# A decoder layer on one core: keys and queries projected for two tiles at a time, in alternate steps

## The reference

```
t  = rms_norm(layer_norm(x)) * rms_w           # self attention, 8 heads of 64
q, k, v = t @ wq, t @ wk, t @ wv
o  = softmax(q k^T / 8, causal) v * sigmoid(t @ w_gates)
x1 = x + o @ wo
x2 = x1 + cross_attention(layer_norm(x1), ctx, mask) @ W_out^T   # 16 heads of 8, tanh-clipped scores
y  = x2 + layer_norm(x2) + experts(...)         # 8 experts, the best 2 of each token
```

## Time and profile before

| what | before |
|---|---|
| median of 3 runs | 259.38 us (257.85 to 260.14) |
| the profiled execution, its own time | 259.18 us |
| its span, first to last instruction | 257.4 us |
| busy PE / PEld / DVE / ACT / POOL | 224.5 / 184.5 / 197.1 / 144.0 / 128.2 us |
| instructions PE / DVE / ACT / POOL | 3360 / 874 / 333 / 184 |
| mean granted TensorE clock | 0.958 |

### The profile page before, as it was taken

The page is one execution under the profiler, slowest core; times in us unless marked ns, Lnnn a source line. Parts: engine busy times, 40 slices in busy tenths (PEclk is TensorE's granted clock), DMA queues, the critical chain, the costliest instruction groups (busy, mean ns, idle before and its releaser), DMA issues. The chain is left out here.

```text
span 257.4 us, 9580 instructions
## 1 busy us (share of the span) xinstructions
PE 224.5 (87%) x3360; PEld 184.5 (72%) x3360; DVE 197.1 (77%) x874; ACT 144.0 (56%) x333; POOL 128.2 (50%) x184
## 2 busy tenths in 40 slices
PE   8888999999999999999999988857987999989800
PEld 2666877886886887877777755436977899989700
DVE  2558687898898889989888897968995777766343
ACT  2455776885776776777667656424332355545400
POOL 1122321413546746646556356636777776656630
PEclk9999999999999999999999999975999999999965
DMA  7995999300000000000000001065774888888376
GB/s 221 254 374 215 401 410 406 135 3 4 3 12 26 14 13 24 14 13 25 13 14 21 16 0 35 24 174 179 218 216 116 268 275 230 268 239 250 94 237 190
DMA packets 24526, 36.31 MB, mean 141 GB/s; under 512 B 3726, under 2 KB 14225, under 8 KB 24224
## 3 DMA queue, kind: packets, MB, share of 16 engines
q1 hardware_dynamic: 20272, 29.98, 36.3%
q0 software_dynamic: 2272, 4.27, 4.7%
q10 hardware_dynamic: 1936, 1.46, 1.9%
HBM read 21.26 MB, written 14.89 MB: 140 GB/s over the span
## 5 line engine op out<-in xcount | busy, mean ns | idle before, releaser
L1959 POOL TENSOR_TENSOR rstd<-var,cst 128x1 f32<-128x1 f32 (+1 forms) x32 | 25.8, 807 | 73.8 <-DVE var L1300 48.7
L2058 POOL DMA_INDIRECT results<-y_sb,meta x39 | 38.3, 981 | 16.9 <-DVE xw_sb L1707 9.1
L505 PE MATMUL six<-gT_sb,gu_sb 128*128 128x128 f32 x312 | 43.3, 288 | 0.6 <-issue 0.6
L505 PEld LDWEIGHTS six<-gT_sb,gu_sb 128*128 128x128 f32 x312 | 39.4, 201 | 1.0 <-issue 0.8
L2016 POOL DMA_INDIRECT slots<-pay,slot_i x32 | 33.2, 1038 | 11.9 <-issue 7.0
L1093 ACT ACTIVATE jsilu<-six 128x256 f32<-128x256 f32 x39 | 14.9, 383 | 21.8 <-PE six L505 21.8
L1690 DVE TENSOR_TENSOR hidT<-jsilu,six 128x256 f32<-128x256 f32 x39 | 16.2, 416 | 10.7 <-PE six L505 10.7
L505 PE MATMUL six<-downT_sb,hidT 128*128 x156 | 23.6, 278 | 0.7 <-DVE hidT L1690 0.7
L1029 ACT ACTIVATE etanh<-six,xscale 128x1024 f32<-128x1024 f32 x16 | 17.8, 1113 | 7.1 <-PE six L505 7.1
L505 PEld LDWEIGHTS six<-downT_sb,hidT 128*128 128x128 f32 x156 | 20.3, 192 | 1.2 <-issue 1.1
L505 PEld LDWEIGHTS six<-wo_sb,oT_sb 128*128 128x128 f32 x128 | 15.5, 191 | 6.4 <-issue 6.4
(11 more groups left out here) (159 smaller groups left out, 537.8 us busy)
## 6 DMA issues: line engine op xcount, KB each, us to landing
gu_sb<-in_guT SPq DMA_DIRECT2D x39, 256.0 KB, 3.7
slots<-empty_sb SPq DMA_DIRECT2D x16, 528.0 KB, 5.9
g_sb<-slots SPq DMA_DIRECT2D x39, 66.0 KB, 3.4
ctxT_all<-in_ctxT SPq DMA_DIRECT2D x1, 1024.0 KB, 8.7
downT_sb<-in_downT SPq DMA_DIRECT2D x1, 1024.0 KB, 9.8
y_all<-results SPq DMA_DIRECT2D x4, 256.0 KB, 3.6
x_all<-in_x SPq DMA_DIRECT2D x2, 320.0 KB, 3.7
results<-y_sb,meta POOLq DMA_INDIRECT x39
```

Source lines behind the costliest of these rows:

```text
L505: return pe.matmul(o, lhsT=l, rhs=r, start=start, stop=stop, **kw)
L1959: nc.gpsimd.tensor_tensor(dst, src, half[:, 0:dst.shape[1]], ALU.pow).then_inc(semaphore, 1)
L2058: nc.gpsimd.indirect_dma_start(results, bass.IndirectOffsetOnAxis(meta[j % (2 * RING)][:, 0:1].bitcast(I32), 0), y_sb[k][:, :], None, boun ...
```

## The change

Two tiles lie side by side in tT_sb ([P, 2, P]), and a product multiplies 128 columns of weights by the 256 columns of both. Fill number n is the keys of tiles n and n+1 where n is even, the queries of tiles n-1 and n where it is odd; step i does fill i+2. So keys and queries alternate from step to step, and each step has four products of 256 columns where it had eight of 128. Half of a fill (two of the four 128-column blocks of weights) goes to ko_bank, half to qp_bank; the two copies of 128 x 512 on ScalarE stay. The loop begins at step -3. `turn_t`, `normalize` and the statistics of x come two steps earlier for the same tile (the statistics now at the ends of odd steps); `turn_t(2)` is put at the end of step -1; the cast of the constants and its wait move from step 0 to -1; the two keep_warm products move to step -2, behind `turn_t(1)`.

TensorE, and the functions that it calls:

```diff
-        tT_sb = several("tT_sb", [P, P])
-        qT_sb = several("qT_sb", [P, NJ, P])
-        k_sb = several("k_sb", [P, NJ, P])
+        tT_sb = several("tT_sb", [P, 2, P])
+        q_sb = several("q_sb", [P, NJ, 2, P], n=2)
+        k_sb = several("k_sb", [P, NJ, 2, P], n=2)
...
-            for i in range(-2, TAIL):
+            for i in range(-3, TAIL):
...
+        def tT(t):
+
+            return tT_sb[t // 2 % BUFS][:, t % 2]
+
+        def query_fill(t):
+
+            return t | 1
...
                 after(pe, t_ready, t)
-                after(pe, egate_ready, t - 1)
+                after(pe, tT_ready, t - 1)
+                after(pe, egate_ready, 0 if t == 2 else t - 3)
                 pe.transpose(tr_ps, t_sb[t % BUFS], ident).then_inc(t_turned, 1)
...
+            def project_pair(n, bank, j0):
+                w = wq_sb if n % 2 else wk_sb
+                both = tT_sb[n // 2 % BUFS].rearrange("p u t -> p (u t)")
+                for m in range(2):
+                    ins = mm(bank[:, m * 2 * P:(m + 1) * 2 * P], w[:, (j0 + m) * P:(j0 + m + 1) * P], both)
+                return ins
+
+            def project_lo(n):
...
+                after(pe, tT_ready, n | 1)
+                after(pe, lo_ready, n - 1)
+                after(pe, oT_ready, n - 3)
+                project_pair(n, ko_bank, 0).then_inc(lo_done, 1)
+
+            def project_hi(n):
+
+                after(pe, hi_ready, n - 1)
+                after(pe, pT_ready, n - 3)
+                after(pe, tanh_ready, n - 4)
+                project_pair(n, qp_bank, NJ // 2).then_inc(hi_done, 1)
...
-                after(pe, qT_ready, t)
-                after(pe, k_ready, t)
+                after(pe, lo_ready, query_fill(t))
+                after(pe, hi_ready, query_fill(t))
...
-                if has(i, -1):
-                    turn_t(i + 1)
+                if has(i, -3) and i != -1:
+                    turn_t(i + 3)
...
-                if i == -1:
+                if i == -2:
                     keep_warm(2, quad[:, 3])
-                if has(i, -1):
-                    project_k(i + 1)
-                    project_q(i + 1)
+                if has(i, -2):
+                    project_lo(i + 2)
+                    project_hi(i + 2)
...
                 if has(i, -1):
                     scores(i + 1)
+                if i == -1:
+                    turn_t(2)
```

ScalarE's step, and its list behind the steps:

```diff
-                if has(i, 0):
-                    evacuate_k(i)
+                if has(i, -1):
+                    evacuate_lo(i + 1)
                 if has(i, 4):
                     turn_xn(i - 4)
-                if has(i, 0):
-                    evacuate_q(i)
+                if has(i, -1):
+                    evacuate_hi(i + 1)
...
-                if has(i, -1):
-                    turn_t(i + 1)
+                if i == 0:
+                    turn_t(2)
+                if has(i, -3) and i != -1:
+                    turn_t(i + 3)
                 if has(i, 0):
                     softmax(i)
...
-            evacuate_q(15)
             turn_xn(11)
-            evacuate_k(15)
```

VectorE's step, and the steps of the statistics:

```diff
-                if i == 0:
+                if i == -1:
                     dve.wait_ge(l_b, 16)
...
-                if has(i, -1):
-                    normalize(i + 1)
+                if has(i, -3):
+                    normalize(i + 3)
...
-XSTEPS = (-1, 0, 2, 4, 6, 8, 10)
+XSTEPS = (-3, -2, 1, 3, 5, 7, 9)
```

More of the change, by code:

```diff
@@ L514, in turn_t @@
                 after(pe, t_ready, t)
-                after(pe, egate_ready, t - 1)
+                after(pe, tT_ready, t - 1)
+                after(pe, egate_ready, 0 if t == 2 else t - 3)
                 pe.transpose(tr_ps, t_sb[t % BUFS], ident).then_inc(t_turned, 1)
-            def project_k(t):
-                if t == 0:
-                    pe.wait_ge(l_wk, 16)
[L522 to L532, removed]
-                    pe.wait_ge(l_wq, 16)
[L534 to L539, removed]
+            def project_pair(n, bank, j0):
[5 more added lines that the diff above has]
+            def project_lo(n):
+                if n == 0:
+                    pe.wait_ge(l_wk, 16)
+                if n == 1:
+                    pe.wait_ge(l_wq, 16)
+                after(pe, tT_ready, n | 1)
[7 more added lines that the diff above has]
+                project_pair(n, qp_bank, NJ // 2).then_inc(hi_done, 1)
             def project_v(t):
@@ L569, in gates @@
                     rows = slice(b * S, (b + 1) * S)
-                    ins = mm(gate_ps[rows], tT_sb[t % BUFS][:, rows], wgate_sb[:, :])
+                    ins = mm(gate_ps[rows], tT(t)[:, rows], wgate_sb[:, :])
                 ins.then_inc(gate_done, 1)
@@ L587, in scores @@
                             rows, cols = slice(a * 64, a * 64 + 64), slice(b * S, (b + 1) * S)
-                            mm(s_ps[cols, a, j], qT_sb[t % BUFS][rows, j, cols],
-                               k_sb[t % BUFS][rows, j, cols], start=(j == 0), stop=False,
+                            mm(s_ps[cols, a, j], q_sb[t // 2 % 2][rows, j, t % 2, cols],
+                               k_sb[t // 2 % 2][rows, j, t % 2, cols], start=(j == 0), stop=False,
                                skip_group_check=True)
@@ L600, in turn_p @@
                 after(pe, weighed, t)
-                if has(t + 1, 0):
-                    after(pe, qT_ready, t + 1)
+                if has(t + 2, 0):
+                    after(pe, hi_ready, t + 2)
                 else:
@@ L615, in attend @@
                 after(pe, v_ready, t)
-                after(pe, k_ready, last(t + 1))
-                if not has(t + 1, 0):
+                after(pe, lo_ready, last(t + 2))
+                if not has(t + 2, 0):
                     after(pe, oT_ready, t - 1)
@@ L686, in turn_a @@
                 after(pe, a_ready, t)
-                after(pe, tT_ready, last(t + 3))
+                after(pe, tT_ready, last(t + 5))
                 after(pe, xnT_ready, t - 1)
@@ L710, in turn_xn @@
                 after(pe, xn_ready, t)
-                after(pe, tT_ready, last(t + 4))
-                if not has(t + 4, 0):
+                after(pe, tT_ready, last(t + 6))
+                if not has(t + 6, 0):
                     after(pe, egate_ready, last(t + 3))
@@ L988, in turn_t, with heads, evacuate_lo, evacuate_hi @@
                 after(act, t_turned, t)
-                nc.scalar.activation(tT_sb[t % BUFS], tr_ps, ACT.Copy,
+                nc.scalar.activation(tT(t), tr_ps, ACT.Copy,
                                      scale=vecs[:, 0:1]).then_inc(tT_ready, 1)
[L993 to L999, removed]
+            def heads(n, j0):
+                pair = (q_sb if n % 2 else k_sb)[n // 2 % 2]
+                return pair[:, j0:j0 + NJ // 2].rearrange("p j u t -> p (j u t)")
+            def evacuate_lo(n):
+                after(act, lo_done, n)
+                copy(heads(n, 0), ko_bank).then_inc(lo_ready, 1)
+            def evacuate_hi(n):
+                after(act, hi_done, n)
+                copy(heads(n, NJ // 2), qp_bank).then_inc(hi_ready, 1)
             def gates(t):
@@ L1017, in turn_p @@
                 after(act, p_turned, t)
-                copy(pT_sb[t % BUFS], qk_ps).then_inc(pT_ready, 1)
+                copy(pT_sb[t % BUFS], pT_ps).then_inc(pT_ready, 1)
             def turn_o(t):
@@ L2021, in x_power @@
             def x_power(i):
-                if i == -1:
+                if i == XSTEPS[0]:
                     pool.wait_ge(l_c, 16)
```

11 lines of the change are left out of this document (5 added, 6 removed).

## The result

The changed kernel takes 267.01 us (median of 4 executions, 263.56 to 269.47), beside 258.91 us for the kernel before on the same chip (257.85 to 260.14). Executions more than 1.5% above the fastest of their kernel, here 268.5 and 269.47 us, do not enter the ratios in this document; the other two, 263.56 and 265.52 us, give a ratio of 1.0216, with a 95% interval of [1.011, 1.0321]. The kernel is slower, as forecast, by more than the 1% that the prediction called its border; whether by 2% the interval leaves open. The forecast time was 262.5 us, the range 259.0 to 265.0: the mean of those two, 264.5 us, lies inside near the top, the median of all four beyond it.

A forecast was written before the change was run, and what follows sets the result against it. TensorE's order was taken to set the pace, VectorE following closely. Lead-in +3.2, steps 1 to 13 -0.9, statistics +1.2 and end -0.2 made +3.3 on 259.18, so 262.5 us, range 259.0 to 265.0 (the forecast's own 261.0 to 264.0).

The forecast's parts named there:

- Lead-in: Before the second scores: two tiles' fills and turns stand ahead on the path, +3.2 us, ends +2.5 and +4.
- Width of a product: TensorE's fills: a record of 256 columns costs what two of 128 cost, 0.215 us, so 1.72 us a step.
- 0.07 a step: Steps 1 to 13: each fill on TensorE 1.72 us instead of 1.79, -0.9 us in all.
- The rival in which the weights set the pace: TensorE's fills: weight loads limit the pace, so wide products make the kernel faster, 256.3 us; chance 7%.
- estimate of 98 ns: TensorE: spacing for 256 columns, between the skill's 81 ns for 128 and 131 for 512; 1.2 times that for 128.
- Statistics of x: Now ahead of even steps on VectorE, delaying turn_xn in steps 6, 8 and 10: +1.2 us, ends 0 and 2.0.
- turn_xn comes 0.40 us late, three times: Steps 6, 8 and 10: 0.81 us of statistics against 0.41 free; cross_attend and values queue behind turn_xn.
- in steps 2 and 4 ... I cost nothing: Steps 2 and 4: no choice of experts stands there, so the moved statistics were costed at nothing.
- The end: Step 14: 1.79 us less TensorE work, but turn_xn waits for VectorE's norm_x, so only -0.2 us.
- The rival in which the delay is given back: Step 14 returns all 1.79 us and the statistics find cover: +0.5, 259.7 us; chance 25%.
- Sum: The whole kernel: +3.2 - 0.9 + 1.2 - 0.2 = +3.3 us, giving 262.5 us.
- The clock rises later: Lead-in: TensorE idle before the clock's rise, first two half fills take twice as long, +1.8, 264.3 us; chance 13%.

The follow-up runs named there:

- lead-in by tile: The changed kernel with its first two fills made for one tile each, by products of 128 columns; 265.56 us, ratio 1.0226.
- combined kernel: The changed kernel with statistics of x at even steps, an unread fill in step 14 and first two fills for one tile each; 262.43 us, ratio 1.0101.
- second profile: The changed kernel run again with nothing changed, profiled at 264.09 us; median 265.1 us, ratio 1.0208.
- place earlier: The changed kernel with VectorE's place written ahead of norm_q instead of behind it; 266.58 us, ratio 1.0206.
- narrow products: The changed kernel with each product of 256 columns done as two of 128 with the same weights; 266.89 us, ratio 1.0309.

## Why the prediction was right in sign and too small

**Lead-in, +3.2 forecast, +3.47 measured: right, step by step.** scores(0) at 12.53 (12.28 forecast), the third fill 2.32 us behind them (2.31), scores(1) at 19.21 (18.93). Most of the 0.25 that is missing lies at the second fill: it begins at 9.78, not 9.60, since the copy that frees its bank starts 0.10 later than reckoned (9.04 against 8.94) and the fill follows the copy's end by 0.14, not 0.05. The lead-in by tile took 1.48 us back where the order was undone, and its profile kept 1.13 of it to the end; in the combined kernel it is not seen at the end.

**Width of a product: right.** A fill takes 69.32 to 71.05 us, from its first product to the next instruction, 1.73 us (1.72 forecast):

```profile
69.32 1.89 PE L512 MATMUL six<-tT_sb,wk_sb 128*128 128x256 f32 x8
71.05 0.27 PE L725 MATMUL turn_bank<-cst,xn_sb 128*128 128x128 f32 x1
```

Eight records in it make 0.216 each, twice the 0.112 of half the width. With the statistics put back the steps up to scores(13) are 0.76 us shorter than before, near the 0.07 a step. The rival in which the weights set the pace is out. The estimate of 98 ns that was worked out from the Trainium skill, "TensorE: Matmul & The Clock Gate", section "Back-to-back issue gap", does not fit either: these float32 records follow each other by 216 ns.

**Statistics of x, +1.2 forecast, 2.4 measured: this term was mis-sized**, above its bound of 2.0 too. What it followed came nearly as written: "turn_xn comes 0.40 us late, three times". Counted from the scores that begin a step, turn_xn starts 0.33, 0.30 and 0.33 us later in steps 5, 7 and 9 than with the statistics at the even steps, and the values queued behind it 0.38, 0.35 and 0.40, together 1.13 of the 1.2. The step that failed is that the prediction stopped there. route, a few products further on, waits for place on the same late VectorE and comes another 0.29, 0.32 and 0.28 us late, 0.89 in all. And "in steps 2 and 4 ... I cost nothing" holds, but step 6, also without a term, is 0.66 us longer, with a wait of 0.56 of the cross attention's scores for VectorE's probs. Less the 0.26 of step 8 this is 1.13 + 0.89 + 0.66 - 0.26 = 2.42. place could have been found in the kernel before, where route once waits 0.2 us for it, in step 13. The size is shown from both sides: by the kernel before with this part alone (2.46 between scores(5) and scores(11)) and by the changed kernel without it (-2.4 in these steps).

**The end, -0.2 forecast, -0.12 at scores(15) and -0.22 at the last instruction from scores(14) on: right.** turn_xn waits 1.46 us for norm_x, and 1.73 us of dead work put there cost 0.70, some 0.4 of them by a wait of the experiment's own. The rival in which the delay is given back is out. In step 13 the changed kernel gains 0.46 that I had not; one part is turn_t, 0.26 us from its start to the next instruction, which no longer stands there as no tile is left to turn.

**Sum.** 3.47 - 0.76 + 2.85 (with the 0.44 in step 4) - 0.46 - 0.22 = 4.88, where +3.3 was forecast and 4.91 profiled. Of the 1.6 that is missing the statistics make 1.2 and the gap in step 4 another 0.44; what the lead-in lost beyond the forecast (0.27) and the fills saved less (0.14) is offset by step 13. That the time still lies inside the stated range is owed to its width, which was drawn for the rivals: the forecast's own range ended at 264.0.

**The clock.** "The clock rises later" did not come as written: in both profiles of the changed kernel the first two fills run at full pace. But the clock took part elsewhere. In the execution profiled with the result it fell to 1.2 GHz from 14.9 us on, behind the first scores, where TensorE had stopped twice for about 0.5 us (before turn_t(3) and before the third fill; the second profile has the same two stops and no fall). The window of the lower clock (length, busy time of PE, granted clock, DMA share, GB/s):

```profile
14.90:18.30 3.40, 3.40 (x10) 0.50 0.99 378
```

The fill in it takes 3.61 us instead of 1.99 from its first start to its last end, and scores(1) come at 20.68 instead of 19.21. Of seven profiles with the changed lead-in two show this fall (the other is the one with place earlier); none of the two with the lead-in by tile does. Behind step 14 a fall is seen in four of the six profiles of the changed order without a fill there, and in none of the three with it. But only two of the four begin right behind the gap of 1.46 us (146.0 with the statistics at the even steps, 149.6 with narrow products). The other two begin some 10 us behind it, after the next turn_xn, and so does a fall of the kernel before with the statistics moved, which has its fills:

```profile
154.10 0.33 PE L715 MATMUL turn_bank<-cst,xn_sb 128*128 128x128 f32 x1 [1.51 <-DVE xn_sb L1306]
```

Its clock stands at 1.2 GHz from 154.7 to 164.9. In seven of the eleven profiles this second turn_xn waits 1.44 to 1.51 us, and in four of these a fall begins within 1.7 us of its start (154.7, 158.3, 158.6, 159.8); in the other four it waits 0.89 to 0.96, and none follows. So every fall between 140 and 170 us stands right behind a gap of some 1.5 us, but of the thirteen such gaps seven have none behind them: the gap alone does not decide, and what else does stays open. Such stretches come on top of the +4.9 of the second profile; how much of the medians they are, executions without a profile can't tell. That the combined kernel's 12 executions lie within 2.7 us, and the changed kernel's 10 within 6.4, fits it.

## What to carry to other kernels

A part of a change that only moves work on the second engine deserves the same care as its headline: follow its delay not to the first instruction that waits for it but to every one up to the end of the step. Here the first was 0.35 to 0.40 us late and a later one another 0.3, and when the later wait was taken away, part of its price came back at the next. Halving the weight loads of products saved nothing here, where a record of twice the width takes twice the time; pairing two tiles is then a matter of order, and its price is the second tile's work ahead of the first result. Time taken off the pacing engine in the last step comes back only as far as the other engine is ready, and the gap of 1.46 us that it left here was followed by the lower clock at once in two of six profiles.

## What was not expected of the hardware

Right behind a gap of some 1.5 us in the midst of full work TensorE could stand at the lower of its two clocks for 3.4, 6.8 or 10.2 us. It happened behind six of thirteen such gaps in these eleven profiles, not behind gaps under 1 us in the same place, and differently in two executions of one kernel: the second turn_xn behind step 14 waited 1.44 us in one profile of the changed kernel and 0.96 in the other, and only the first has the fall there. With the gap of step 14 filled by products that nobody reads, the same 3.4 us held 98 records instead of 48, and that profiled execution was 1.39 us shorter; that the fill was the cause is likely and not shown, since the clock also stayed up in four profiles with that gap open.
